# Second cross attention and expert projections of a fused transformer kernel: products of the first expert layer placed between the score units

## The reference

```python
x = x + L0_xattn(_layernorm(x), ctx)          # self attention, cross attention, FFN 256-1024-256
x = x + L0_ffn(_layernorm(x))                 # the "linear branch": x @ (W + low rank).T + b
x = x + L1_xattn(_layernorm(x), ctx, masks)   # the second cross attention: 16 heads of 16, 77 keys
x = x + L1_ffn(_layernorm(x))                 # gated experts

def _L1_xattn_ref(query, key, value, pad_mask, subsq_mask, Wq, bq, ...):
    att = einsum('bhsd,bhtd->bhst', q, k) / sqrt(16)   # masked to -1e9 by both masks
    return einsum('bhst,bhtd->bhsd', softmax(att), v)

def _L1_ffn_ref(x, ...):
    n1 = _layernorm(x, ln1_w, ln1_b)
    rw = _gating(n1.reshape(b * t, c), smha_sim, smha_gates, 2)   # weights of 8 experts per row
    q = einsum('btc,ech,bte->bth', n1, q_proj, rw)     # k and v likewise: the "products"
    # causal attention, output projection by expert, then a second gated expert layer
```

## Time and profile before

| | us |
|---|---|
| median of 3 runs | 1312.76 |
| lowest, highest | 1309.76, 1315.47 |
| profiled execution | 1300.66 |
| its span | 1298.9 |

### The profile page before, as it was taken

The page is one execution under the profiler, slowest core; times in us unless marked ns, Lnnn a source line. Parts: engine busy times, 40 slices in busy tenths (PEclk is TensorE's granted clock), DMA queues, the critical chain, the costliest instruction groups (busy, mean ns, idle before and its releaser), DMA issues. The chain is left out here.

```text
span 1298.9 us, 19730 instructions
## 1 busy us (share of the span) xinstructions
PE 1133.6 (87%) x7004; PEld 772.5 (59%) x7004; DVE 837.4 (64%) x1820; ACT 562.0 (43%) x1207; POOL 253.0 (19%) x418
## 2 busy tenths in 40 slices
PE   8788999888878789879867778899999888899999
PEld 4343333333333338757643435799988677689988
DVE  5577777877755678757663757765545466865555
ACT  6206666655656455465333554200013333543442
POOL 5012222222220046444100024000010112400000
PEclk9879999989979889999987865899999999999999
DMA  7840373330534611007438000001030000000000
GB/s 218 204 98 2 58 65 50 50 51 2 103 49 73 121 47 25 1 8 88 73 62 186 3 2 1 1 1 33 1 130 1 1 1 1 1 17 1 17 17 17
DMA packets 50768, 61.04 MB, mean 47 GB/s; under 512 B 16474, under 2 KB 40560, under 8 KB 50032
## 3 DMA queue, kind: packets, MB, share of 16 engines
q1 hardware_dynamic: 50672, 59.79, 23.2%
HBM read 44.02 MB, written 15.15 MB: 46 GB/s over the span
## 5 line engine op out<-in xcount | busy, mean ns | idle before, releaser
L669 PE MATMUL PS<-ARENA 128*17 128x512 f32 (+14 forms) x1720 | 296.9, 444 | 46.5 <-DVE ARENA L1970 14.8
L1502 ACT ACTIVATE ARENA<-PS 128x512 f32<-128x512 f32 (+3 forms) x384 | 169.9, 495 | 135.3 <-PE PS L669 133.1
L1970 DVE TENSOR_REDUCE ARENA<-PS 128x1 f32<-128x128 f32 (+7 forms) x256 | 183.0, 752 | 46.3 <-PE PS L669 44.5
L669 PEld LDWEIGHTS PS<-ARENA 128*17 128x17 f32 (+5 forms) x1720 | 87.2, 100 | 193.5 <-issue 105.0
L669 PE MATMUL PS<-WQKVP,TRR 128*128 128x384 f32 x512 | 136.0, 347 | 0.7 <-DVE ARENA L2227 0.7
L669 PE MATMUL PS<-ARENA,W 128*128 128x128 f32 (+2 forms) x398 | 96.8, 501 | 29.5 <-ACT ARENA L1603 14.2
L2418 POOL TENSOR_SCALAR_AFFINE_SELECT ARENA<-ARENA 128x128 f32<-128x128 f32 x256 | 74.8, 302 | 224.1 <-ACT ARENA L1502 222.2
L669 PEld LDWEIGHTS PS<-W2P,INT 128*128 128x128 f32 x768 | 94.8, 188 | 2.8
L669 PE MATMUL PS<-W2P,INT 128*128 128x256 f32 x768 | 95.5, 279 | 0.0
L669 PEld LDWEIGHTS PS<-WQKVP,TRR 128*128 128x128 f32 x512 | 93.9, 194 | 1.3 <-DVE ARENA L2227 1.1
L2386 POOL TENSOR_TENSOR rstd<-var,halves 128x4 f32<-128x4 f32 x36 | 38.3, 1063 | 288.5 <-DVE var L1757 178.0
(11 more groups left out here) (249 smaller groups left out, 2017.6 us busy)
## 6 DMA issues: line engine op xcount, KB each, us to landing
ARENA<-qk_parts SPq DMA_DIRECT2D x96, 128.0 KB, 5.4
ARENA<-xq_parts SPq DMA_DIRECT2D x48, 128.0 KB, 5.7
ARENA<-yq_parts SPq DMA_DIRECT2D x48, 128.0 KB, 5.4
qk_parts<-ARENA SPq DMA_DIRECT2D x6, 768.0 KB, 3.3
ARENA<-in_w SPq DMA_DIRECT2D x2, 2048.0 KB, 11.2
xq_parts<-ARENA SPq DMA_DIRECT2D x8, 384.0 KB, 2.7
yq_parts<-BC SPq DMA_DIRECT2D x8, 384.0 KB, 2.7
ARENA<-in_wqkv SPq DMA_DIRECT2D x1, 3072.0 KB, 19.3
```

Of the source, the lines that this page charges most:

```text
L669: return nc.tensor.matmul(o, lhsT, rhs, start=start, stop=stop, **kw)
L1502: ins = nc.scalar.activation(PROB[GRP * (step % 2) + j][:, 0:w], PS[:, uses[key][0], 0:w], ACT.Exp, scale=HD ** -0.5)
L1970: ins = v.tensor_reduce(negm[:, n % 2, TPB * j + st:TPB * j + st + 1], PS[:, bank:bank + 2, :].rearrange("p b s -> p (b s)")[:, 0:P * (st ...
```

## The change

1. **Order of the plan.** `expert_plan` now walks the ticks of `expert_ticks`: 64 score slots, three tail steps, and products between them. From slot 44 on three products follow every two slots, 30 in all, three more stand between the tail steps, then come the other 95. Products count as ticks, so the chains' offsets (`CHAIN`, 23 ticks from `add` to `softmax`) run over them; `plain` (ScalarE's normalising) stands in two halves behind `lean`. While a product's tile is one of the first five it takes bank 2 or 3 only, later banks 2 to 7 in turn; `narrow()` gives the other steps bank 0 or 1 once products have begun. `turn_qk` starts behind the last `add`.
2. **FFN loop.** It has five steps. In step 4 the maxima of chunk 0 stand ahead of the turn of the linear branch, `second_turn(0)` right behind it, two mask turns ahead of the context values; the filler is 6 matmuls in place of 24. Chunk 3's normalising, transposes, queries and their splits move into slots 5 to 15 of the plan, the other mask turns into slots 16 and 17.
3. **Maxima.** Chunk 1's stand in slots 4 to 7 (before 0 to 7), chunk 2's in 20 to 27 (16 to 23), chunk 3's in 34 to 41 (30 to 37); the turns in slots 9, 29 and 43 (10, 26 and 41).
4. **Pack of chunk 2.** It lies in four pieces of four heads in `H` and `TR` (`YLATE`) instead of two of eight in `ARENA`, so `load_second(2)` issues 24 transfers and `load_second_rows` 12.
5. **Weights.** Two transfers of half the weights, the first after the last `lin`, the second after the context values. GpSimd casts and subtracts, two slots per expert from slot 31; ScalarE's casts go.

```diff
+def early_slots():
+    for c, first, every, turn in ((1, 4, 2, 9), (2, 20, 1, 29), (3, 34, 1, 43)):
+        for m in range(8):
+            put(first + m // every, "max2", c, m % 4, m // 4)
+        put(turn, "neg2", c)
+    put(5, "late_norm", 3)
+    for half in range(2):
+        put(7 + half, "late_turn", 3, half)
+        put(10 + half, "late_q", 3, half)
+        put(11 + half, "late_rest", 3, half)
+        put(13 + half, "late_mid", 3, half)
+        put(14 + half, "late_low", 3, half)
+        put(16 + half, "hide", 2 + half)
+    for e in range(EXPERTS):
+        put(FIRST_WEIGHT + 2 * e, "weights", e)
...
+def expert_ticks():
+    products = [("product", i, e) for i in range(TILES) for e in range(EXPERTS)]
+    tail = [("pv2", XSTEPS - 1), ("end", XSTEPS - 2), ("end", XSTEPS - 1)]
+    done = 0
+    for k in range(4 * XSTEPS):
+        yield "slot", *divmod(k, GRP)
+        if k >= FIRST_PRODUCT:
+            wanted = min(3 * (k + 1 - FIRST_PRODUCT) // 2, EXPERTS * EARLY_TILES)
+            while done < wanted:
+                yield products[done]
+                done += 1
+    for op in tail:
+        yield op
+        yield products[done]
+        done += 1
+    yield from products[done:]
...
+        def pack_pieces(c, g):
+            if c == 2:
+                return [(GRP * k, GRP, YLATE[2 * g + k]) for k in range(2)]
+            return [(0, HH, YPACK[c][g])]
...
         def load_second_rows(eng, c):
             eng.wait_ge(ymparts_ready, c + 1)
             for g in range(2):
-                for r in range(3):
+                for h0, heads, pack in pack_pieces(c, g):
+                    first = 32 * g + 4 * h0
+                    for r in range(3):
...
                     elif op == "product":
-                        bank = 4 + (EXPERTS * n + e) % 4
+                        banks = (2, 3) if n < EARLY_TILES else (2, 3, 4, 5, 6, 7)
+                        bank = banks[products % len(banks)]
...
+                if s == 4:
+                    for m in range(8):
+                        second_maximum(0, m % 4, m // 4)
                 if 0 < s < 5:
-                    turn("t_lin", "lin", H, s - 1, wait=(0, 24, 6, 6, 24)[s])
+                    turn("t_lin", "lin", H, s - 1, wait=(0, 24, 6, 6, 6)[s])
+                if s == 4:
+                    second_turn(0)
...
                 if s == 4:
+                    turn_mask(0)
+                    turn_mask(1)
                     context_values()
-                    for m in range(8):
-                        second_maximum(0, m % 4, m // 4)
-                if 0 < s < 5:
+                if 0 < s < 4:
                     turn("t_xat", "xat", H, s - 1)
...
                 elif op == "weights":
-                    pool.wait_ge(wqkv_upper, n + 1)
-                    g.tensor_tensor(WQKVP[1][:, :, n, :], WQKV[:, :, n, :], WQKVP[0][:, :, n, :].bitcast(F32),
-                                    ALU.subtract).then_inc(wqkv_split, 1)
+                    loaded(pool, "wqkv")
+                    split(WQKV[:, :, n, :], WQKVP[0][:, :, n, :], WQKVP[1][:, :, n, :], wqkv_split)
```

More of the change, by code:

```diff
@@ L277, in cross_plan @@
             yield (op, *at)
[L280 to L297 removed]
+FIRST_PRODUCT, FIRST_WEIGHT, EARLY_TILES = 44, 31, 5
@@ new lines, with put @@
+CHAIN = {1: [("stat_x", 0)], 2: [("stat_x", 1)], 4: [("lean",)], 5: [("plain", 0)], 6: [("plain", 1)], 7: [("stat", 0)], 8: [("stat", 1)],
+         9: [("center", 0)], 10: [("center", 1)], 12: [("scale", 0)], 13: [("scale", 1)], 14: [("turn_n1", 0), ("square", 0)],
+         15: [("turn_n1", 1), ("square", 1)], 17: [("lower", 0)], 18: [("lower", 1)], 19: [("logits",)], 20: [("gate",)],
+         22: [("softmax",)]}
+CHAIN_LENGTH = 23
+def early_slots():
+    slots = {}
+    def put(at, *op):
+        slots.setdefault(at, []).append(op)
+    for c, first, every, turn in ((1, 4, 2, 9), (2, 20, 1, 29), (3, 34, 1, 43)):
+        for m in range(8):
+            put(first + m // every, "max2", c, m % 4, m // 4)
[10 more added lines that the diff above has]
+        put(FIRST_WEIGHT + 2 * e, "weights", e)
+    return slots
@@ L305, in add @@
         if t % 4 == 3:
+            chains[t // 4] = p
             yield "add", t // 4
[L308 to L337 removed]
@@ new lines, in expert_plan @@
+    slots, chains, turned = early_slots(), {}, 0
+    for p, (kind, n, *at) in enumerate(expert_ticks()):
+        if kind == "product":
+            e = at[0]
+            assert n // 4 in chains and p >= chains[n // 4] + CHAIN_LENGTH
+            yield "product", n, e
+            if len(chains) == 4 and turned < n and e % 2 == 0 and (turned < n - 1 or e >= 2):
+                yield "turn_qk", turned
+                turned += 1
+        elif kind == "slot":
+            j = at[0]
+            if j == 3 and n > 0:
+                yield "evac2", n - 1
+            yield "score2", n, j
+            if j == 1 and n > 0:
+                yield "pv2", n - 1
+            if j == 2 and n >= 2:
+                yield from add(n - 2)
+            yield from slots.get(GRP * n + j, [])
+        elif kind == "pv2":
+            yield "pv2", n
+        elif n == XSTEPS - 2:
+            yield from add(n)
+            yield "evac2", n + 1
+        else:
+            yield from add(n)
+        for c, first in list(chains.items()):
+            for name, *half in CHAIN.get(p - first, []):
@@ L1634, in _ @@
             loaded(act, "bk3")
-            for s in range(6):
+            for s in range(5):
                 if s < 4:
```

271 lines of the change are left out of this document (134 added, 137 removed).

## The result

| | before | after |
|---|---|---|
| median of 4 runs each, us | 1311.26 | 1296.29 |
| lowest, highest | 1307.66, 1315.47 | 1289.56, 1300.99 |
| profiled execution, us | 1300.66 | 1289.56 |

The changed kernel takes 0.9897 of the time (95% interval 0.9849 to 0.9945), 15 us less. I had forecast 31 less: the sign and the range held, the size did not.

The account below looks back on a forecast made before the run. TensorE, 87% busy, was taken as the bound, with room for products among the last score slots. Stages running to -10, -11, -9, +14 and finally -31 us took 1312.76 to 1282 us, range 1262 to 1302.

Parts of the forecast that it names:

- Stage 1: Up to the first score: it comes at 666 instead of 676.4, -10 us (bounds -15, -8).
- Stage 2: Score slots 0 to 31: 55.9 us becomes 55, -1, with slot 32 at 721.
- The new wait at slot 32: Slot 32 waits 7.5 us (bounds 5 and 12) for chunk 2's rows of maxima, sent in 12 transfers.
- Stage 3: Score slots 32 to 43: 23.4 us becomes 26, slot 44 at 747, together -9.
- Stage 4: Slots 44 to 63 and the tail, with 33 products: 70 us (bounds 62, 90), +22.5, together +14.
- The 58: Stage 4: TensorE's work at full clock, 33 products included, takes 58 us.
- These are 12 us: Stage 4: three gate waits, two half-clock dips and dense norm chains add 12 us to TensorE's work.
- By their order the splits end before product 0 needs them: Stage 3: GpSimd's weight splits finish before the first product; a norm chain's power waits for one split at most.
- two such: Stage 4: two half-clock stretches, each behind a logits step and losing 1.5 us.
- Stage 5: The 95 products left after stage 4: 110 us, to 927, in place of 154.8 for 128; -45.
- Rival A: Stage 4 serialised: VectorE's chain steps wait for ScalarE and GpSimd, products behind them; 86 us, 1298 in all; chance 0.19.
- the 1285 us: Stage 3: total if every centring, scaling and lowering met a GpSimd split, costing 6 us in place of 1.

Follow-up runs that it names:

- second profile: The changed kernel itself, unedited, run again on the same chip as the kernel with all six edits: 1296.40 us, 0.9924 of the time before.
- splits: Changed kernel with GpSimd's eight weight splits in score slots 30 to 37, one a slot, in place of 31, 33 to 45: 1288.40 us in one execution.
- turn: Changed kernel with the turn of chunk 3's maxima in slot 42 in place of 43: 1301.12 us in one execution.
- rows: Changed kernel where a score step waits only for the three rows of maxima of its own piece of the pack: 1299.57 us in one execution.
- rows and order: Changed kernel with a semaphore for each piece of rows, and chunk 3's pack loaded ahead of chunk 2's rows: 1283.56 us in one execution.
- banks of the context values: Changed kernel where the two context value steps ahead of the first score write banks of ring 0 to 3, not 6 and 7: 1295.21 us in one execution.
- third bank: Changed kernel with early products in banks 2, 3 and 7, and scores from slot 43 on in 4 and 5: 1278.48 us in one execution.
- gate: Changed kernel with VectorE's gate in two parts in neighbouring places of the plan, ScalarE's exponential at the second: 1299.61 us in one execution.
- all six: Changed kernel with weight splits, turn, rows, pack order, two-part gate and third-bank edits together: 1278.89 us, 0.9787 of the time before.
- weights later: All six edits, with the second half of the weights issued between the halves of chunk 2's rows and splits in slots 31 to 38: 1278.66 us, 0.9767 of before.

## Why the prediction was wrong

**Stage 1** was undersized: -10, measured -13.6. The order came as I read it, but the context values ran at full clock (1.90 us) and the first score too (0.38), where I took half clock from the row behind an idle stretch.

**Stage 2** held: 55.9 to 55, measured 56.4, in the second profile 59.6. The new wait at slot 32 was 8.72 for 7.5, its cause the twelve issues; the wait for chunk 2's pack was 0.90 for 2. Not foreseen were the 3.50 us of the third score, which takes the bank that VectorE empties only behind the linear branch's sums and statistics. With such a wait missing from the sum, that it came within 1.4 us is partly luck.

**Stage 3**: 26, measured 27.9.

**Stage 4** is the step that failed: "These are 12 us", on top of 58. The 58 were right in every kernel (57.6 to 61.7 at full clock). The 12 were 28.7:

| stage 4, us | length | idle | lost to half clock |
|---|---|---|---|
| forecast | 70 | 9 | 3 |
| changed kernel | 87.4 | 16.7 | 12.0 |
| the same, second profile | 87.3 | 16.6 | 12.0 |
| splits | 81.6 | 12.5 | 9.0 |
| turn | 83.4 | 13.7 | 9.1 |
| rows | 84.1 | 15.6 | 9.6 |
| rows and order | 81.0 | 15.5 | 6.5 |
| banks of the context values | 82.2 | 12.5 | 9.8 |
| third bank | 78.3 | 11.3 | 9.4 |
| gate | 80.1 | 14.4 | 6.6 |
| all six | 70.9 | 7.9 | 1.3 |
| weights later | 72.8 | 8.3 | 3.2 |

8.98 of the idle is the wait of the first product, which the forecast put "near 750". Behind it stands one sentence: "By their order the splits end before product 0 needs them, and the power waits for one split at most." The splits did end in time for the products. But I asked only what the splits do to a power, not what a power does to the splits, and put their whole effect on VectorE into stage 3 (my sum for stage 4 even takes 3 us off for them). In the plan's own order the last three stand in slots 41, 43 and 45, behind chunk 1's power, and the gate stands in slot 42. They came down on it, and TensorE, through the turn's bank, and ScalarE both stood behind the gate. The splits experiment prices this: stage 4 is 5.8 us shorter without them, of the 17.4 us that it took over the forecast; a third bank gives 9.1, all six edits 16.5. For the other two gates the wait was right (2.83 and 2.30 for 2.3), though the forecast does not say how 4.3 us of gate and 3.4 us of other work make 2.3. The other part is half clock: 12.0 us for "two such" dips of 1.5. It stood behind nearly every long wait; with the waits gone (all six edits) it cost 1.3 us in all. The stage then took 70.9 us, near the 70 that I had forecast for it. Which wait costs how much half clock is not shown: the rows and order kernel lost 6.5 us with as much idle time as the rows kernel, which lost 9.6.

**Stage 5** held: 110, measured 109.

**Rival A** gives the time that came (86 us for the stage, 1298 in the end), not quite the mechanism: it had VectorE's steps waiting for ScalarE and GpSimd in turn through both chains. What the runs show is one long gate, a ring of two banks, and the clock.

**Behind the last product** I had forecast nothing. The only profile of before takes 340.9 us there, the thirteen others 342.6 to 347.6, with equal instructions and 1.7 us of the changed kernel's 3.3 at one wait for the second norm (2.8 us for 1.1). Whether the change does that stays open; before has one profile.

One sum in the forecast is off by its own terms: the 1285 us for splits beside every step of stage 3 should be 1287 (6 us in place of 1).

## What to carry to other kernels

When an engine's work is moved into another's queue, walk that queue to its end, including the steps that wait for third engines: what stands behind such a step comes down later, all at once, on whatever runs then, and a chain of small steps is held up longest for its size. Price a wait in a stretch of small work with its half clock, here 0.4 to 0.8 us for each us of idle while the waits were long. And a product ring that is emptied by an engine with blocks of 4 us needs banks for that block: one more bank brought more here (9.7 us from slot 32 to the last product) than any change of order (7.5 at most), by one profile each.

## What the runs showed of the hardware

A VectorE step of 128x4 elements took 1.47 us, and one of 128x32 with one input 1.77, beside GpSimd subtractions of 1.80 and 1.86; 0.16 and 0.17 with GpSimd idle. Row transfers of 4 KB take 0.62 us of SyncE each, as those of 8 KB do; they land in 1.8 to 1.9 us on quiet DMA engines and in 4.8 behind 3 MB of weights and pack. And two executions of one kernel differ by 3.3 us at slot 20 behind one and the same wait of 3.50 us: half clock lasted from 667.68 to 671.2 us in the first and from 677.18 to 687.4 in the second.
